# Graph network on one core: in the heads stage, GpSimd makes the radial half of each message and the own-row term, and VectorE makes the shares one group ahead

## The reference, cut to what matters

```python
proj = jnp.einsum('nf,hfg->nhg', x, w_proj)          # 4 heads
delta = proj[sender] - proj[receiver]
def seg_softmax_msg(logits):
    ...
    e = jnp.exp(logits - m[receiver])
    s = jax.ops.segment_sum(e, receiver, num_segments=num_nodes)
    alpha = e / s[receiver]
    return jax.ops.segment_sum(alpha[:, :, None] * delta, receiver, num_segments=num_nodes)
out = seg_softmax_msg(radial_logits) + seg_softmax_msg(tangential_logits)
out = jnp.nan_to_num(out.mean(axis=1))
return x + out @ w_out                               # then x = layernorm(x + this)
```

## Time and profile before

| | |
|---|---|
| median of 3 runs | 2980.59 us (2978.1 to 2980.78) |
| the profiled execution | 2978.72 us |
| its span, first to last instruction | 2976.6 us |
| mean granted TensorE clock | 0.743 of 2.4 GHz |
| heads stage in it | 1344.8 to 1429.6 us, 84.8 us |
| busy over the span: VectorE, GpSimd | 2084.0 us, 1784.8 us |

### The profile page before, as it was taken

One profiled execution on the slowest core, in us unless ns is written; L12 is line 12 of the kernel. 1 busy time (PEld: TensorE's weight loads), 2 busy tenths in 40 slices (PEclk: granted clock), 3 DMA queues, 4 the chain that ended last, 5 costly groups with the idle time before them and its releaser, 6 DMA issues. The chain is left out here.

```text
span 2976.6 us, 64648 instructions
## 1 busy us (share of the span) xinstructions
PE 2220.9 (75%) x13922; PEld 1706.0 (57%) x13923; DVE 2084.0 (70%) x7853; ACT 632.3 (21%) x1180; POOL 1784.8 (60%) x1866
## 2 busy tenths in 40 slices
PE   0288988889898898885799557667677676676748
PEld 0155555555555555555799446656666565566637
DVE  6477777777777777746466557777777777777755
ACT  0323322233322233231000111111111111111100
POOL 0077777777777777730001167777777777777722
PEclk6599999999999999995899555555555555555558
DMA  1144554545545454542000133333333333333330
GB/s 42 51 127 130 143 141 129 142 128 142 140 134 142 127 142 132 141 92 58 20 1 2 35 74 83 80 82 81 81 81 83 80 82 81 82 81 81 81 42 12
DMA packets 425510, 268.62 MB, mean 90 GB/s; under 512 B 334069, under 2 KB 375908, under 8 KB 425444
## 3 DMA queue, kind: packets, MB, share of 16 engines
q0 software_dynamic: 71040, 176.52, 23.5%
q1 hardware_dynamic: 284418, 49.42, 8.7%
q10 hardware_dynamic: 69986, 41.88, 4.6%
HBM read 231.16 MB, written 15.97 MB: 83 GB/s over the span
## 5 line engine op out<-in xcount | busy, mean ns | idle before, releaser
L906 POOL DMA_INDIRECT edges_rows<-table,edges_idx x888 | 863.7, 973 | 294.7 <-issue 231.4
L2073 POOL DMA_INDIRECT all_arena<-table_kv,edges_idx x888 | 855.5, 963 | 276.5 <-issue 256.7
L2265 PE MATMUL edges_acc<-edges_values,edges_into 128*128 128x136 f32 x1776 | 511.6, 461 | 261.1 <-DVE edges_values L2153 244.7
L2265 PEld LDWEIGHTS edges_acc<-edges_values,edges_into 128*128 128x128 f32 x1776 | 416.6, 328 | 308.6 <-DVE edges_values L2153 295.0
L1062 PE MATMUL edges_radial_ps<-edges_rows,edges_into_w 128*128 x1776 | 460.9, 396 | 91.6 <-SPq L916 73.2
L975 DVE TENSOR_SCALAR edges_cell<-edges_ramp,edges_strip_key,first_key 128x400 bf16<-128x400 f16 x1184 | 451.3, 381 | 0.0
L1062 PEld LDWEIGHTS edges_radial_ps<-edges_rows,edges_into_w 128*128 128x128 f32 x1776 | 319.8, 190 | 215.9 <-issue 175.4
L2118 DVE TENSOR_SCALAR edges_ahead<-edges_nodes,edges_starts,edges_dst_f 128x128 bf16<-128x128 f32 x894 | 262.4, 359 | 172.7 <-issue 172.7
L974 DVE TENSOR_SCALAR edges_low<-edges_places,first_src_low 128x128 bf16<-128x128 bf16 x1184 | 330.6, 279 | 0.0
L2199 ACT COPY edges_into_t<-edges_t_ps 128x384 bf16<-128x384 bf16 x298 | 142.6, 479 | 874.4 <-PE edges_t_ps L2233 868.6
L1057 PE MATMUL edges_cells_ps<-edges_cell,edges_low 128*128 128x400 bf16 x1184 | 251.4, 335 | 36.2 <-DVE edges_cell L975 29.9
(11 more groups left out here) (344 smaller groups left out, 2555.8 us busy)
## 6 DMA issues: line engine op xcount, KB each, us to landing
edges_values<-in_edge_attr SPq DMA_DIRECT2D x888, 32.0 KB
all_arena<-all_arena ACTq DMA_DIRECT2D x50, 400.0 KB
edges_rows<-table,edges_idx POOLq DMA_INDIRECT x888
all_arena<-table_kv,edges_idx POOLq DMA_INDIRECT x888
edges_attr<-in_edge_attr ACTq DMA_DIRECT2D x51, 256.0 KB
edges_bias<-bias_kept SPq DMA_DIRECT2D x296, 12.0 KB
bias_kept<-edges_bias_out ACTq DMA_DIRECT2D x52, 64.0 KB
table<-all_arena SPq DMA_DIRECT2D x1, 3250.0 KB, 11.4
```

The source lines that it names most:

```text
L906: pool.indirect_dma_start(rows[:, n, :], None, table0, bass.IndirectOffsetOnAxis(ap=idx[:, n:n + 1], axis=0)).then_inc(s_rows[g], 16)
L2073: pool.indirect_dma_start(rows[:, n, :], None, table_kv, bass.IndirectOffsetOnAxis(ap=idx[:, n:n + 1], axis=0)).then_inc(s_rows[g], 16)
L2265: last = nc.tensor.matmul(acc[:, 0:2 * F + H2], into[:, h, j, :], values[:, h, j, :], start=False, stop=True, skip_group_check=True)
```

## The change

GpSimd gets a function `half_message(g)`: it multiplies the radial sums by their shares into `msg`, and makes the own-row term into a new double buffer `less`. VectorE loses these two instructions. What is left of `message(g)` begins with the tangential product, then makes the shares of the next group (`shares(g + 1)`), then waits for GpSimd's half, and does the two additions. Two semaphores are new: `s_share` (VectorE to GpSimd) and `s_half_msg` (back).

```diff
 @block.gpsimd
+    def half_message(g):
+        i = g % 2
+        pool.wait_ge(s_share, g + 1)
+        if g >= 2:
+            pool.wait_ge(s_mps, g - 1)
+            pool.wait_ge(s_msg, g - 1)
+        pool.tensor_tensor(msg[:, i].rearrange("p n (h f) -> p n h f", f=F),
+                           rad[:, i, :, 0:2 * F].rearrange("p n (h f) -> p n h f", f=F),
+                           share[:, i, 0].unsqueeze(3).broadcast_to([P, 2 * U, 2, F]), ALU.mult)
+        pool.tensor_tensor(less[:, i], x[:, blocks(g), :], over(twice[:, blocks(g)], F), ALU.mult).then_inc(s_half_msg, 1)
+
+    half_message(0)
+    half_message(1)
     pool.wait_ge(s_deg, 1)
     pool.partition_all_reduce(deg_top[:, 1:2], deg_top[:, 0:1], P, RMAX).then_inc(s_deg_all, 1)
-    for g in range(GR):
+    for g in range(2, GR):
+        half_message(g)
+        rstd_group(pool, st, g - 2, s_var, s_rstd)
+    for g in range(GR - 2, GR):
         rstd_group(pool, st, g, s_var, s_rstd)
 @block.vector
+    def shares(g):
+        i = g % 2
+        here = by_pair[:, 2 * U * g:2 * U * (g + 1), :]
+        if g == 0:
+            dve.wait_ge(s_ld, 32)
+        dve.wait_ge(s_rads[i], 16 * (g // 2 + 1))
+        if g >= 2:
+            dve.wait_ge(s_half_msg, g - 1)
+        dve.tensor_scalar(share[:, i, 0], rad[:, i, :, 2 * F:PAIR], TINY, None, ALU.max)
+        step(dve.tensor_scalar(share[:, i, 1], here[:, :, 2 * F:PAIR], TINY, None, ALU.max))
+        dve.reciprocal(share[:, i], share[:, i]).then_inc(s_share, 1)
+        dve.wait_ge(s_share, g + 1)
     def message(g):
-        if g == 0:
-            dve.wait_ge(s_ld, 32)
-        dve.wait_ge(s_rads[i], 16 * (g // 2 + 1))
-        if g >= 2:
-            dve.wait_ge(s_mps, g - 1)
-        dve.tensor_scalar(share[:, i, 0], sums[:, :, 2 * F:PAIR], TINY, None, ALU.max)
-        step(dve.tensor_scalar(share[:, i, 1], here[:, :, 2 * F:PAIR], TINY, None, ALU.max))
-        step(dve.reciprocal(share[:, i], share[:, i]))
-        dve.tensor_tensor(own[:, :, :], x[:, blocks(g), :], over(twice[:, blocks(g)], F), ALU.mult)
-        dve.tensor_tensor(twos(to), twos(sums[:, :, 0:2 * F]),
-                          share[:, i, 0].unsqueeze(3).broadcast_to([P, 2 * U, 2, F]), ALU.mult)
-        step(dve.tensor_tensor(twos(here[:, :, 0:2 * F]), twos(here[:, :, 0:2 * F]),
-                               share[:, i, 1].unsqueeze(3).broadcast_to([P, 2 * U, 2, F]), ALU.mult))
+        dve.tensor_tensor(twos(here[:, :, 0:2 * F]), twos(here[:, :, 0:2 * F]),
+                          share[:, i, 1].unsqueeze(3).broadcast_to([P, 2 * U, 2, F]), ALU.mult).then_inc(s_ch, 1)
+        step.n += 1
+        if g + 1 < GR:
+            shares(g + 1)
+        dve.wait_ge(s_ch, step.n)
+        dve.wait_ge(s_half_msg, g + 1)
         step(dve.tensor_tensor(to, to, here[:, :, 0:2 * F], ALU.add))
-        dve.tensor_tensor(four, four, own[:, :, :].unsqueeze(2).broadcast_to([P, U, H0, F]), ALU.add).then_inc(s_msg, 1)
+        dve.tensor_tensor(four, four, less[:, i].unsqueeze(2).broadcast_to([P, U, H0, F]), ALU.add).then_inc(s_msg, 1)
+    shares(0)
     message(0)
```

More of the change, by code:

```diff
@@ L1185, in build @@
                 own = ph.sb("own", [P, U, F])
+                less = ph.sb("less", [P, 2, U, F])
+                s_share, s_half_msg = ph.sem("s_share"), ph.sem("s_half_message")
                 y = ph.sb("y", [P, U, F])
```

## The result

| | before | changed |
|---|---|---|
| median of 15 runs | 2980.62 us | 2986.25 us |
| ratio, 95% interval | | 1.0022 (1.0014 to 1.0030) |
| profiled execution: span | 2976.6 us | 2984.4 us |
| heads stage in it, from VectorE's first instruction | 84.75 us | 89.01 us |

The change costs 5.6 us by the medians; 7.0 was forecast. The stage itself accounts for 4.26 us in the profile. Its start moved too (1344.88 to 1348.98). In the eleven profiles taken later, of kernels that edit nothing ahead of the stage, the start lies between 1344.05 and 1352.77, and in the second profile of the kernel of before it was 1345.46. From here on all times of the stage count from its start, so that they can be compared: the kernel of before took 84.74 us there the second time, and the one experiment that was profiled twice took 85.96 and 85.90.

What follows compares the result with a forecast made beforehand. VectorE was taken to bound the heads stage up to `message(4)`, with a 24.4 us chain behind. Delays of 3.3, 3.6, 6.5, 6.8 and 7.0 us by message gave +7.0 us, 2987.5 us on the median, range 2980 to 2993.

Steps and rivals of the forecast that it cites:

- VectorE and GpSimd take turns: Heads stage: each excludes the other for its whole instruction with two SBUF inputs; own case, +7.0 us, 45%.
- The reverse case: VectorE coming second to a running GpSimd instruction: taken to wait too, though one product took 0.51 us for 0.49.
- No exclusion: Rival: GpSimd's half runs freely beside VectorE in the heads stage; about -1 us, 2979.6 us; 13%.
- VectorE goes first: Rival: GpSimd gives way whenever VectorE has an instruction with two SBUF inputs; +8.1 us, 2988.7 us; 15%.
- What GpSimd pays: GpSimd's half: 2.36 us for the product, 0.72 us for the own-row term, 3.1 us a group, five times.
- GpSimd is dearer: Rival: GpSimd's product costs 2.9 to 3.43 us; +9.7 to +12.4 us, 2990 to 2993 us; 15%.
- Message 0: First message: GpSimd's products let in ahead of VectorE's additions; ends at 1363.2 for 1359.89, 3.3 us late.
- Message 1: Second message: VectorE stands 1.6 us for the refill of `rad`; ends at 1370.6 for 1367.00, 3.6 us late.
- Message 2: Third message: VectorE idle 5.3 us for GpSimd's half 2 behind the reduction; 6.5 us late, the largest term.
- the other order that gave +6.4: GpSimd's half 1 whole before VectorE's second addition in message 0; reduction starts 1.2 us sooner, +6.4 us.
- The rival by which the second configuration holds nothing: GpSimd's half 2 follows the reduction at once, there at 1374; +1.8 us, 2982.4 us; 10%.
- Messages 3 and 4: Last two messages, with GpSimd's product and own-row term in the path: 6.8 and 7.0 us late.

Runs made afterwards that it cites:

- the one experiment that was profiled twice: Changed kernel with both products and own-row term back on VectorE, only the shares made a group ahead; stage 85.96 and 85.90 us, ratio to before 1.0006.
- e1: Changed kernel with GpSimd's product and own-row term replaced by fills that read nothing; stage 82.20 us, ratio to before 0.9994.
- e10: Changed kernel with GpSimd's product of the radial half made twice in every group, a wait between; stage 103.91 us, one run.
- e2: Changed kernel with the reduction across partitions replaced by a copy, configuration instructions gone; stage 91.98 us, ratio to before 1.0030.
- e8: Changed kernel with the reduction replaced by a copy and the radial sums' refill allowed once GpSimd's half has read them; stage 87.63 us, ratio to before 1.0028.
- e9: As e5, but GpSimd makes the own-row terms of groups 2 to 4 ahead of all powers; stage 84.48 us, ratio to before 0.9996.
- e3: Changed kernel with SyncE's refill of the radial sums waiting on GpSimd's half, not the whole message; stage 90.20 us, ratio to before 1.0021.
- e5: Kernel of before with only the own-row term moved to GpSimd, each later group's ahead of a power; stage 84.91 us, ratio to before 1.0003.
- e7: Kernel of before with the own-row term made by ScalarE in place of VectorE; stage 84.98 us, ratio to before 0.9997.

## Why the prediction was right

**That VectorE and GpSimd take turns** was inferred from three stretched instructions and was the step that decided: e1 shows it from the one side (message 0 ends 3.84 us earlier without reading), e10 from the other. The reverse case, which I had called nearly unseen, is in messages 0 and 4, at the clamp of message 2 and at the end of new_x(0) and new_x(1): VectorE stands for the whole rest of GpSimd's instruction. Message 1 met none of GpSimd's work, and none of its instructions was longer than 1.49 us. "No exclusion" and "VectorE goes first" are both out; at three of the meetings GpSimd, going from one instruction to the next, was let in ahead of a VectorE instruction that its semaphore had just released (1361.99 ahead of 1362.17, 1391.54 ahead of 1391.59). The Trainium skill (SBUF — State Buffer, Who interferes with whom) has a lock on the shared ports, and the trace agrees: 3.50 us for 1.49 beside a GpSimd product. Its remark that a GpSimd instruction which only writes doesn't hold one with two inputs agrees with e1, 1.49 us beside a fill.

**What GpSimd pays** was 2.36 us in the sum, and 2.32 to 2.34 where it met nobody, so the rival "GpSimd is dearer" is out. The estimate of 2.8 us, worked out from a figure of the Trainium skill (GPSIMD Engine Reference, Elementwise — side-by-side cycle accounting), is too high for this form, and the measurement decides.

**Message 0** was 3.3 late in the sum and came 3.61 late, as GpSimd's own-row term of half 1 was let in ahead of VectorE's second addition as well. **Message 1**: 3.6 in the sum, 4.30 measured; the wait for the refill was 2.5 us where the sum had 1.6, since the load landed 4.1 us behind the end of message 0 and not 3.7.

**Message 2 is the term that was mis-sized.** "Half 2: 1363.8 + 14.2 = 1378.0 ... VectorE stands idle 5.3 us and ends the message at 1384.1 ... 6.5 late": it was 4.06 late, and VectorE lost 2.4 us to half 2 and not 5.3. Half 1 was ready 1.7 us sooner, as its own-row term went ahead of the second addition (the other order that gave +6.4 in the sum), and the pause was 12.98 us and not 14.2. So half 2 was 2.6 us earlier than in the sum, which the prediction itself had named as a sign of being wrong. The pause isn't a constant: 13.0, 14.2 and 15.4 us in three profiles of kernels with the same halves around it. As a cause it was overrated: e2 shows that without it GpSimd's half finds the next additions to hold up, and only with the early refill of e8 does message 2 end 2.4 us sooner. The rival by which the second configuration holds nothing is out in the change, with 6.61 us behind the reduction; ahead of e1's fill there was no such wait.

**Messages 3 and 4** were to add 0.3 and 0.2 and added 0.2 and nothing. **The tail** of 24.4 us was 24.37.

The sum for the stage was +7.0 and it measured +4.26. The medians differ by 5.6, and the interval of the ratio is 4.2 to 8.9 us. So between nothing and 4.7 us lie outside the stage, in parts that aren't edited, though the prediction had said that none of these would take another time; which parts, no run shows. In the one profile the stage began 4.1 us later than before. Whether that is scatter isn't shown: the starts of one and the same kernel differ by 1.9 us. The forecast of the time came out nearer than its own sum deserved, and that is luck. The prediction gave 0.57 to a loss of more than 0.2%, and the measured 0.22%, with an interval from 0.14 to 0.30, lies on that line.

## What to carry to other kernels

Work moved from VectorE to GpSimd is only gone where VectorE waits or is in an instruction that doesn't need what GpSimd holds. Elsewhere it comes back at GpSimd's price (here 2.33 us for 1.48), so look at what VectorE runs at that moment before counting what it sheds. In a stage in which several engines follow one another closely, one engine's relief came to little here: 2.5 us taken off VectorE left the stage 0.3 us shorter at best (e9). Measure such an edit by the stage's own length, which repeated within 0.1 us for two kernels where the whole time scattered by several microseconds. And when an experiment takes a cost away, look for what else it took: e1 removed a wait of 6.6 us together with the reading.

## What the runs showed of the hardware that was not expected

- Some instructions of VectorE with one input were held too: a clamp of 20 elements took 2.30 us beside a GpSimd product, and 1.10 us beside a fill that reads nothing; a cast of 2 numbers took 1.25 us beside a fill. Others were not: the reciprocal of 40 elements kept its 0.40 us, and a comparison of one element its 0.15 us, beside the own-row term. What tells them apart, no run here was made to show.
- The pause of GpSimd around one reduction was 12.98 us in the change, 14.24 in e3 and 15.39 in e10. In e1, with a fill behind the reduction, only the wait ahead of it was there, 7.33 us.
- The same 20 matmul instructions took 2.44 us or 4.53 us, at a granted clock of 1.00 or 0.50, according to the kernel and alike in two profiles of one kernel; that is 2.1 us on the path of new_x(0), more than any of the edits e5, e7 and e9 gained.
